# A projection cut into four parts between four tiles of weighing, in layer 2 of a four-layer network

## The reference, cut to what matters

```python
qkv = x @ qkv_w.T + qkv_b                      # q, k, v per place
k_nb = kk[:, :, ni][:, :, :, :, nj]            # 7 x 7 neighbours of each place, clipped at the border
v_nb = v[:, :, ni][:, :, :, :, nj]
attn = einsum('bnijd,bniajcd->bnijac', q * scale, k_nb) + bias
attn = softmax(attn.reshape(b, nh, h, w, k * k), axis=-1)
out = einsum('bnijac,bniajcd->bnijd', attn, v_nb)
out = out @ proj_w.T + proj_b
```

## Time and profile before

| | |
|---|---|
| time, median of 3 runs | 3279.31 us (3275.99 to 3297.35) |
| the profiled execution | 3278.58 us, its span 3276.8 us |
| layer 2 in that span | about 2012 to 2520 us |
| TensorE busy, whole span | 2988.0 us (91%), granted clock 0.965 |
| DVE, ACT, POOL busy | 2141.9 (65%), 1994.0 (61%), 1130.3 us (34%) |

### The profile page before, as it was taken

The page is one execution under the profiler, slowest core; times in us unless marked ns, Lnnn a source line. Parts: engine busy times, 40 slices in busy tenths (PEclk is TensorE's granted clock), DMA queues, the critical chain, the costliest instruction groups (busy, mean ns, idle before and its releaser), DMA issues. The chain is left out here.

```text
span 3276.8 us, 103102 instructions
## 1 busy us (share of the span) xinstructions
PE 2988.0 (91%) x43288; PEld 1649.1 (50%) x43288; DVE 2141.9 (65%) x5155; ACT 1994.0 (61%) x4348; POOL 1130.3 (34%) x1441
## 2 busy tenths in 40 slices
PE   8999999999996999999999987999898788888886
PEld 3333333333323555556565655667675555555554
DVE  6878778878864677767677643555554466656664
ACT  3667676666664555565556524555554677777774
POOL 3433433433321222222222211322222555555543
PEclk9999999999997999999999988999998899999997
DMA  7777777788672233233323214555553333333332
GB/s 224 160 172 159 169 174 170 152 183 182 137 181 87 64 87 81 67 91 89 88 71 96 67 46 139 183 165 157 171 161 111 90 89 109 115 116 120 117 104 79
DMA packets 298892, 411.55 MB, mean 126 GB/s; under 512 B 39328, under 2 KB 255808, under 8 KB 277824
## 3 DMA queue, kind: packets, MB, share of 16 engines
q1 hardware_dynamic: 276720, 272.65, 27.6%
q0 software_dynamic: 18000, 131.08, 20.1%
q10 hardware_dynamic: 3712, 1.23, 0.2%
HBM read 219.47 MB, written 53.81 MB: 83 GB/s over the span
## 5 line engine op out<-in xcount | busy, mean ns | idle before, releaser
L863 ACT ACTIVATE l_sizes<-l_probs 128x2048 f32<-128x2048 f32 x256 | 487.1, 1908 | 299.1 <-DVE l_probs L804 290.0
L1946 ACT ACTIVATE l_logits<-l_logits,l_low 128x100 f32<-128x100 f32 x1024 | 372.7, 366 | 210.0 <-DVE l_low L1926 209.7
L1953 POOL TENSOR_TENSOR l_logits<-l_logits,l_inv 128x400 f32<-128x400 f32 x256 | 242.4, 948 | 736.3 <-DVE l_inv L1932 733.9
L301 PE MATMUL l_psum<-shared_x,shared_space 128*128 128x512 f32 x896 | 411.2, 604 | 12.6 <-DVE l_row_var L1499 10.7
L804 DVE TENSOR_TENSOR l_probs<-l_psum,l_decay 128x1024 f32<-128x1024 f32 x256 | 299.7, 1219 | 84.9 <-PE l_psum L678 75.7
L804 DVE TENSOR_TENSOR l_probs<-l_psum,shared_space 128x1024 f32<-128x1024 f32 x256 | 300.3, 1219 | 73.3 <-PE l_psum L678 72.8
L678 PE MATMUL l_psum<-l_qk 32*128 32x512 f32 x2048 | 340.0, 645 | 5.3 <-DVE l_qk L763 2.1
L972 POOL DMA_DIRECT2D l_sizes<-l_sizes x125 | 108.7, 869 | 536.3 <-ACT l_sizes L863 524.2
L1743 POOL TENSOR_TENSOR shared_space<-shared_space,l_causal 128x1024 f32<-128x1024 f32 x64 | 153.0, 2392 | 361.0 <-DVE l_x_act L1441 210.9
L693 PE MATMUL l_psum<-l_probs,shared_x 128*32 128x512 f32 x2048 | 270.9, 601 | 0.2
L301 PEld LDWEIGHTS l_psum<-shared_x,shared_space 128*128 128x128 f32 x896 | 163.5, 191 | 199.7 <-issue 192.8
(11 more groups left out here) (246 smaller groups left out, 5770.5 us busy)
## 6 DMA issues: line engine op xcount, KB each, us to landing
l_sizes<-l_sizes POOLq DMA_DIRECT2D x125, 1024.0 KB, 7.6
l_V_windows<-v_image SPq DMA_DIRECT2D x512, 100.0 KB
l_V_windows<-v_padded SPq DMA_DIRECT2D x512, 100.0 KB
shared_space<-rows_c SPq DMA_DIRECT2D x64, 512.0 KB, 5.9
shared_x<-y SPq DMA_DIRECT2D x24, 1024.0 KB, 5.9
y<-l_res SPq DMA_DIRECT2D x30, 512.0 KB, 3.3
l_e_everywhere<-rows_e SPq DMA_DIRECT2D x112, 128.0 KB, 5.7
y<-shared_x SPq DMA_DIRECT2D x17, 512.0 KB, 3.7
```

Of the source, the lines that this page charges most:

```text
L301: i = nc.tensor.matmul(out, w[:, k, m * P:(m + 1) * P], act[:, k, n0:n1], start=(k == 0), stop=(k == tiles - 1))
L863: nc.scalar.activation(sizes[:, slot(N), :, :], probs[:, N % 2, :, :], ACT.Abs).then_inc(sized, 1)
L1946: nc.scalar.activation(e, e, ACT.Exp, scale=-1.0, bias=self.low[:, N % 4, i:i + 1], accum_out=self.total[:, N % 4, i:i + 1]).then_inc(self ...
L1953: nc.gpsimd.tensor_tensor(p, p, self.inv[:, N % 4, :].unsqueeze(2).to_broadcast([P, STEP, NKEY]), ALU.mult).then_inc(self.p_ready, 1)
```

## The change

On TensorE the step becomes: scores (even steps), turn of step `N - 2`, the waits of the weighing, and then four times one tile's weighing (16 instructions) followed by one part of the projection. Values and queries have four parts (values one token block and one half of the channels in each; queries a quarter of the columns in each). Keys and output have two, behind the first and the third tile; nothing follows the second and the fourth. In `n` = 4 the second output unit stays whole and ahead of the turn, and the values of the next image are interleaved. The mean of the group norm in `n` = 1 moves from ahead of the turn to the end of the step. The loops of the other engines stay as they are.

```diff
+                def part(name, q):
+                    kind, b = name[0], name[1]
+                    out = ring.region(name)
+                    if kind == "v":
+                        half, late, k = name[2] // 2, q == 0, q % HALVES
...
+                        i = nc.tensor.matmul(out[:, q // HALVES * C:(q // HALVES + 1) * C], xn[:, k, t * P:(t + 1) * P],
+                                             wqkv[:, k, 2 * C:3 * C], start=(k == 0), stop=(k == HALVES - 1))
...
+                    elif q % 2:
+                        return
+                    elif kind == "k":
+                        half, m, k = name[2] // 2, HALVES + name[2] % 2, q // 2
...
+                def unit_at(b, n):
+                    if n < 2 and b < B:
+                        return ("q", b, 1, n)
+                    if n == 3 and 0 < b < B:
+                        return ("out", b - 1, 1, 0)
+                    if 4 <= n < 14 and b + 1 < B:
+                        return ("v", b + 1, n - 4) if n < 8 else ("q", b + 1, 0, n - 8) if n < 10 else ("k", b + 1, n - 10)
+                    if n >= 14 and b < B:
+                        return ("out", b, 0, n - 14)
+                    return None
...
-                    if n in (3, 4) and 0 < b < B:
-                        project_out(b - 1, 1, n - 3)
...
-                    if n >= 14 and b < B:
-                        project_out(b, 0, n - 14)
+                    if n == 4 and 0 < b < B:
+                        project_out(b - 1, 1, 1)
                     if 2 <= N < B * STEPS + 2:
                         w.turn(nc, pe, N - 2)
+                    name = unit_at(b, n)
                     if N >= 3:
-                        w.weigh(nc, pe, N - 3)
+                        w.may_weigh(pe, N - 3)
+                    for i in range(STEP):
+                        if N >= 3:
+                            w.weigh_tile(nc, N - 3, i)
+                        if name is not None:
+                            part(name, i)
+                    if n == 1 and b < B:
+                        norm.average(nc, pe, ring, b + 1)
```

More of the change, by code:

```diff
@@ L1899, in turn, with may_weigh @@
         m.then_inc(self.turned, 1)
-    def weigh(self, nc, pe, N):
+    def may_weigh(self, pe, N):
         pe.wait_ge(self.pt_ready, N + 1)
@@ L1905, in weigh, with weigh_tile @@
             pe.wait_ge(self.o_copied, HALVES * (N // (STEPS // 2)))
-        for i in range(STEP):
[L1907 to L1917, removed]
+    def weigh_tile(self, nc, N, i):
+        _, tr, tc = self.tile(N, i)
+        for g in range(HALVES):
+            for a in range(4):
+                h = 4 * g + a
+                out = self.ps[a * HD:(a + 1) * HD, (4 + g) * BANK:(5 + g) * BANK].rearrange("p (r c) -> p r c", c=SIDE)
+                r0 = tr % 4 * TILE
+                m = nc.tensor.matmul(out[:, r0:r0 + TILE, tc * TILE:(tc + 1) * TILE],
+                                     self.v[0:NKEY, N % self.slots, i, h * HD:(h + 1) * HD],
+                                     self.pt[0:NKEY, N % 2, i * P + self.place(N, h) * 16:i * P + (self.place(N, h) + 1) * 16],
+                                     start=True, stop=True)
+        if i == STEP - 1:
+            m.then_inc(self.weighed, 1)
+    def weigh(self, nc, pe, N):
+        self.may_weigh(pe, N)
+        for i in range(STEP):
+            self.weigh_tile(nc, N, i)
     def add_and_low(self, nc, dve, N, adds, gain):
@@ L2129, in _ @@
                 pe.wait_ge(rest_loaded, 112)
+                def part(name, q):
[3 more added lines that the diff above has]
+                        half, late, k = name[2] // 2, q == 0, q % HALVES
+                        if late and b > 0:
+                            pe.wait_ge(xn_ready, 4 * (b - 1) + 2 * half + 2)
+                        if late:
+                            ring.may_fill(pe, name)
+                        t = 2 * name[2] + q // HALVES
+                        i = nc.tensor.matmul(out[:, q // HALVES * C:(q // HALVES + 1) * C], xn[:, k, t * P:(t + 1) * P],
+                                             wqkv[:, k, 2 * C:3 * C], start=(k == 0), stop=(k == HALVES - 1))
+                    elif kind == "q":
+                        half, g = name[2], name[3]
+                        if q == 0:
+                            if b > 0:
+                                pe.wait_ge(xn_ready, 4 * (b - 1) + 2 * half + 2)
+                            ring.may_fill(pe, name)
+                        for k in range(HALVES):
+                            band = xn[:, k, (4 * half + q) * P:(4 * half + q + 1) * P]
+                            i = nc.tensor.matmul(out[:, q * P:(q + 1) * P], wqkv[:, k, g * P:(g + 1) * P],
+                                                 band.rearrange("p (r t c) -> p t r c", r=TILE, c=TILE), start=(k == 0),
+                                                 stop=(k == HALVES - 1))
+                    elif q % 2:
+                        return
+                    elif kind == "k":
+                        half, m, k = name[2] // 2, HALVES + name[2] % 2, q // 2
+                        if q == 0:
+                            if b > 0:
+                                pe.wait_ge(xn_ready, 4 * (b - 1) + 2 * half + 2)
+                            ring.may_fill(pe, name)
+                        i = nc.tensor.matmul(out, wqkv[:, k, m * P:(m + 1) * P], xn[:, k, half * BANK:(half + 1) * BANK],
+                                             start=(k == 0), stop=(k == HALVES - 1))
+                        if k == HALVES - 1:
+                            i.then_inc(ring.filled(name), 1)
+                        return
+                    else:
+                        half, m, k = name[2], name[3], q // 2
+                        if q == 0:
+                            pe.wait_ge(w.o_copied, 4 * b + 2 * half + 2)
+                            ring.may_fill(pe, name)
+                        i = nc.tensor.matmul(out, wo[:, k, m * P:(m + 1) * P], OT[:, k, half * BANK:(half + 1) * BANK],
+                                             start=(k == 0), stop=(k == HALVES - 1))
+                        if k == HALVES - 1:
+                            i.then_inc(ring.filled(name), 1)
+                        return
+                    if q == 3:
+                        i.then_inc(ring.filled(name), 1)
```

## The result

The changed kernel takes 3346.49 us (median of 4 runs, 3343.74 to 3350.88) against 3281.91 for the kernel before (4 runs): ratio 1.020, 95% interval 1.0163 to 1.0238, slower by 65 us. The forecast was 3361 us, 3310 to 3405. The profiled execution took 3343.74 us with a span of 3341.9.

What follows compares the result with a forecast made beforehand. TensorE was taken to set the pace. The terms 52.2 + 30.6 + 10.5 + 6.4 - 2 - 15 = 82.7 us, on the profiled 3278.58 us, gave 3361 us, 2.5% slower, range 3310 to 3405.

Steps and rivals of the forecast that it cites:

- Items 1 and 2: Added return trips between full array and tiles, 0.30 us each: values and queries +52.2 us, keys and output +30.6 us.
- item 8: TensorE's clock in layer 2: no change taken; bounds 10 us gained or 26 us lost.
- Item 3: DVE copies the turned block after keys and output, so 15 weighings wait 0.7 us each: +10.5 us.
- Item 4: The weighing of step 11 waits 0.9 us for ACT's copy in 7 images: +6.4 us.
- Item 5: The turn ahead lies in step 3's wait for ACT's copy: -2 us; elsewhere POOL's result is in time, nothing.
- Item 6: TensorE's stops without releaser in runs of scores and weighing mostly go: -15 us.
- Item 7: SP and the windows of values: the gather is at most one step later, needed eight steps on: nothing.
- the clock gives way: Rival: added gaps bring TensorE to 1.2 GHz for a quarter of the layer, 63 us more, 3424 us; chance 0.11.
- the trips are free: Rival: items 1 and 2 vanish since loads and starts are hidden; 3258 us, not slower; chance 0.09.
- DVE becomes the pace in all key and output steps: Rival: all 51 such steps wait 0.7 us, 36 us instead of 10.5; 3386 us; chance 0.10.

Runs made afterwards that it cites:

- e3: The changed kernel, but DVE copies the turned block before it takes keys or output and before the moments; 3330.99 us, ratio 1.014.
- e6: As e3, but in step 11 the four parts of the keys stand whole ahead of the weighing's waits; 3341.76 us, ratio 1.0162.
- e7: As e4, but in even steps the scores stand between the weighing and the projection; 3310.61 us, ratio 1.008.
- e5: The changed kernel with eight parts instead of four for the queries, in the 28 query steps that have a weighing; 3384.48 us, ratio 1.031.
- e1: Against the kernel before, turn and weighing stand ahead of the projection, which stays whole; 3300.0 us, ratio 1.0059.
- e4: As e1, but DVE copies the turned block before it takes keys or output; 3275.02 us, ratio 0.9977.
- e8: The kernel of e4 once more, on the same chip as e7 and with five rounds; 3270.65 us, ratio 0.9979.

## Why the prediction was right

The sign, the size and the mechanism held; the sum, 82.7 us, was 18 us above the measured difference of the totals and 7 above that of layer 2. Item by item, by the numbers of the forecast:

- *Items 1 and 2, the trips*, 82.8 us. PE's busy time grew by 76.4. The price of 0.30 was right where it was read (0.31 measured). Too high was the last trip of key and output steps: behind tiles the four transposes take 0.64 us against 0.60 behind a projection, so not 0.11 but 0.04 of load is bare there, 51 x 0.07 = 3.6 us; and the two query steps at the layer's very start have no weighing between their parts, 1.8 us. The even steps, which the forecast left out, add about 0.1 us each behind values and queries, by estimate 3 us in all; and the 5 us that the clock gave back (item 8) are in the 76.4.
- *Item 3, DVE's late copy*, 10.5 us in 15 waits of 0.7. Measured 10.7 in 17, the 15 at 0.62 us; e3 shows most of it on the path.
- *Item 4, ACT's copy in step 11*, 6.4 us. In step 11 the waits are 6.8 us; e6 takes them away, though its total doesn't confirm the gain.
- *Item 5, the turn ahead*, -2 us. In step 3 the wait for ACT fell from 1.6 us to 0.97, 4.5 us in seven images. That is more than the turn's 3.7, because in six of them the turn itself first waits 0.35 to 0.49 us for POOL, 2.75 us in all. Both together are 1.8 us less than before. The turn doesn't cover all of itself since ACT's copy ends later, as the forecast had it: about 2.1 us behind the start of the last weighing of step 2 in most images, where it was 1.5 to 2.0. Elsewhere POOL's waits are 2.0 us against 2.4: nothing, as forecast. e7 shows how thin this cover is.
- *Item 6, stops without releaser*, -15 us. 27.8 to 12.4 us over all lines: -15.4. They went where the forecast said, as the rows of the last image from its step 5 on show, where most steps have no projection (answering to the earlier trace rows):

```profile
PE l_psum L1915 <- issue: 4.3, 3, 2.3
PE l_psum L1886 <- issue: 3.4, 3, 1.8
```

That is 7.7 us where there were 8.1. Outside these steps 19.7 us became 4.7, and 3.3 in e3 and 2.0 in e5. What makes them stays open: e1, with unbroken weighings, has 7.9 us outside the last image, e4 and e8 have 13 and 14, and e7, whose runs are the longest, 17.
- *Item 7, the windows of values*, nothing. No wait of TensorE for them shows.
- *Item 8, the clock*, no change. 0.97 became 0.98: stretches at 1.2 GHz add up to 34 us before and to 24 now, so some 5 us were gained, and 20 of the 24 us lie in the last image. The rival "the clock gives way" is out: 276 added gaps of 0.1 to 0.2 us do not lower it.

So the waits came out about even, and the layer's 75.4 us are its changes of kind. The rival "the trips are free" is out by the timeline and by e5; that DVE becomes the pace in all key and output steps is out by 17 waits instead of 51. One sum of the forecast is off: the bounds that it lists give 3316 to 3411 us and not 3310 to 3405; the result lies in both. The price of the rival on the clock, 63 us, holds for 127 us spent at 1.2 GHz; 127 us of work at full clock would cost 127 more.

The rule of the Trainium skill, "TensorEngine Tiling (Array Packing)", section "Tiling Modes", that a change of tiling mode drains TensorE, agrees with the rows read here, at 0.10 and 0.09 us for the two directions. The 0.11 us of load is no part of that rule.

## What to carry to other kernels

Work with small tiles of the array and work over the whole array are each cheap in long runs; count the changes between them before cutting either, at the price read from one such place in the trace (0.3 us a return trip here). The price hides in busy time, so compare busy time at an equal number of instructions. When a producer moves ahead on one engine, move its consumer ahead on the next engine too: DVE's copy, left behind keys and output, made TensorE wait 10.7 us here and 34.9 in e1, and once moved the waits were gone (e3, e4).

## What the runs showed of the hardware that was not expected

Small gaps on TensorE did not lower the granted clock here: it is 0.98 with 276 added trips and with 388 (e5), and 0.97 before. What does lower it stays open. The lowest, 0.93, went with 34.0 us of waits for POOL of up to 2.0 us each (e7), but e1 has 34.9 us of waits for DVE of up to 1.7 us and 0.98, and one and the same kernel shows 0.97 (e4) and 0.95 (e8).

The execution time of the untouched layers ahead moves by up to 15 us from run to run (layer 2 begins at 1997.4 us in e4 and at 2012.8 before), so differences of 0.3% of this kernel are better read from the layer's own stretch. That has a spread of its own: e4 and e8 differ in it by 5.9 us.
